# Rounding to eight bits on unscaled values in a fused attention and feed-forward kernel: block floors and limits in bf16, and set places for GpSimd's sums

## The chip, the cores and the metric

The kernel runs on one core of a Trainium2 chip. The metric is the device time of the whole program in microseconds (us); less is better. The engines of the core run at the same time, each through its own list of instructions in order, and wait for each other at semaphores: TensorE (PE), VectorE (DVE), ScalarE (ACT), GpSimd (POOL) and the queue of SyncE (SP), which issues most transfers.

## The reference, cut to what matters

```python
x = x + attn(cond(x, weights, itok_B_0_15), Wqkv, bqkv, Wo, bo)    # x: 64 x 32 x 512
x = x + ffn(gated(x, itok_B_9_3973, conv_w), weight, bias)

# cond: each batch's 32 channels mixed by one of 16 matrices; attn: softmax over 32 tokens
# gated: a mean over the first `length` columns, 5 taps over the rows, gate = sigmoid, x * gate
def quantize_mx(x2d):                       # rows in blocks of 32 values
    amax = jnp.max(jnp.abs(xb), axis=-1)
    exp = jnp.floor(jnp.log2(jnp.maximum(amax, 1e-38))) - 8
    scale = jnp.exp2(exp)                   # a power of two for each block
    q = jnp.clip(xb / scale[..., None], -448.0, 448.0).astype(jnp.float8_e4m3fn)
    return q, scale
out = dequant(quantize_mx(x)) @ dequant(quantize_mx(weight)).T + bias   # then cast to bf16
```

## The kernel before, in words

The 2048 rows of x (64 batches of 32 channels) are 16 tiles of 128 rows and 512 columns. Two tiles make a unit, so there are eight units (UNITS = 8, SUB = 2). The quantising code works in ten steps, numbered v: v = 0 and 1 are the two halves of the feed-forward weight, v = 2 to 9 are the units 0 to 7.

All engines follow one loop over s that is written out by hand. In pass s, TensorE works on the attention of unit s, the projections of unit s + 1, the mixing of unit s + 2 and the feed-forward product of unit s - 2. Its order in a pass is: transposes of step s, `turn_v(s)`, `project_qk(s + 1, 0)`, `attend(s)`, `mix(s + 2)`, `project_out(s, 0)`, `project_qk(s + 1, 1)`, `project_out(s, 1)`, `scores(s + 1)`, `ffn(s - 2, 0)`, `project_v(s + 1)`, `convolve(s)`, `ffn(s - 2, 1)`. Three of its waits matter here: `attend(s)` (L481) waits for the four transposes `softmax_turn` of VectorE; `project_out(s, 1)` (L498) waits for `x2_done`, VectorE's first `residual_sum` (L855) of the unit, because both halves use one PSUM bank; `convolve(s)` (L505) waits for both `masked_sum` (L864) of VectorE.

ScalarE's order in a pass begins `copy_v(s)`, `magnitude(s + 1, 0)`, `copy_o(s)`, `magnitude(s + 1, 1)`, `copy_transposed(s)`. `copy_o` (L663) waits for `attend`. Before the first pass its order is two `copy_mix`, then `magnitude(0, 0)` and `magnitude(0, 1)`.

Quantising a step before the change: VectorE takes the largest magnitude of each block (`block_max`, L878), multiplies it by the gate (`gated_max`), keeps its exponent bits (`scale_exponent`), makes the block scale (`scale_value`, L916) and its inverse (`scale_inverse`, L923), multiplies the inverse by the gate (`gated_inverse`, L929) and writes the scaled values h (`scaled`, L941). ScalarE writes 2^20 |h| in bf16 (`magnitude`, L656). VectorE rounds h by adding max(2^20 |h|, floor) and taking it away again (`round_sum`, L950; `round_back`, L958), clips (`clip`, L967), and GpSimd multiplies by the block scale (`dequantise`, L373), which gives xq. TensorE transposes xq.

GpSimd has three kinds of sums besides: `bias_low` (L386), `residual` (L363, x plus a bias row, 128 x 1024 in f32) and `final_sum` (L294). In pass s its order is `residual(s)`, `dequantise(s + 1)`, `final_sum(s - 2, 0)`, `final_sum(s - 2, 1)`.

VectorE's matrix for the five taps (`band_matrix`, L801 to L818) lies between `scaled(0, ...)` and `round_sum(0, 0)`. `score_max(0)` (L825) follows the second weight half's `block_max` and scales, and `softmax_inverse(0)` follows it.

## Time and profile before

| | |
|---|---|
| median of 3 runs | 169.82 us (169.04 to 169.82) |
| the profiled execution's own time | 170.97 us |
| its span, first to last instruction | 169.3 us |
| mean granted clock of TensorE | 0.879 of 2.4 GHz |
| busy: PE, DVE, ACT, POOL | 130.5, 134.9, 65.4, 64.6 us |

An engine's busy time counts what its instructions last, waits inside an instruction too. Where an instruction lasts much longer than others of its line and shape, it waited for something after it had been started. A clock of 1.00 is 2.4 GHz and 0.50 is 1.2 GHz. "issue" in the chain is time in which the engine on the chain had nothing that the profile shows as its releaser.

### The profile page before, as it was taken

The numbers are of one execution on the slowest core, as the hardware profiler recorded it, in microseconds if no ns is written. First come the engines' busy times: TensorE is split into PE (matmuls) and PEld (weight loads), VectorE is DVE, ScalarE is ACT, GpSimd is POOL, SyncE is SP. The second block draws the span as 40 slices with busy tenths as digits, with TensorE's granted clock in tenths as the row PEclk, the third lists the DMA queues.
The fourth block names the chain that finished last, engine by engine and source line by source line (L and its number), as shares of the span: only waits on it lengthen the run. The fifth ranks groups of instructions, "written<-read, shape, count | busy, mean of one in ns | idle before, by whom it ended". The sixth has DMA issues, their size and how long they took to land.

```text
span 169.3 us, 2698 instructions
## 1 busy us (share of the span) xinstructions
PE 130.5 (77%) x738; PEld 90.4 (53%) x738; DVE 134.9 (80%) x279; ACT 65.4 (39%) x158; POOL 64.6 (38%) x48
## 2 busy tenths in 40 slices
PE   6902899699679889959994999499929955947492
PEld 2402789586477676647573867376716633323130
DVE  4198299759987989899989797978799699599932
ACT  0110433554552646426451545144523463106321
POOL 5330058005612902580555055505551553254500
PEclk9985559999978999999999699959995996587959
DMA  4979103040400000042016001100110011101033
GB/s 112 330 216 321 41 15 122 4 129 6 129 8 2 0 0 0 12 148 98 4 64 187 9 3 64 62 0 0 66 62 0 0 62 62 46 18 41 25 124 124
DMA packets 9489, 11.49 MB, mean 68 GB/s; under 512 B 3954, under 2 KB 4466, under 8 KB 9474
## 3 DMA queue, kind: packets, MB, share of 16 engines
q1 hardware_dynamic: 7186, 8.62, 15.2%
q10 hardware_dynamic: 2096, 2.64, 4.9%
q0 software_dynamic: 192, 0.05, 0.5%
q8 instruction: 6, 0.10, 0.2%
q14 instruction: 9, 0.07, 0.2%
HBM read 7.12 MB, written 4.19 MB: 67 GB/s over the span
## 4 chain that ended last, share of the span: by engine, by line
PE 65%; issue 13%; DVE 6%; DMA 5%; POOL 3%; ACT 3%; SPq 2%; POOLq 1%; ACTq 0%; DVEq 0%
PE ps_qk L439 17%; PE ps_mix L426 12%; PE ps_wo L498 10%; PE ps_v L450 8%; PE ps_ffn L535 7%; DMA mix_w<-in_L_cond_weights_dram 5%; PE ps_att L481 3%; POOL xq L373 2%; PE ps_ffn L533 2%; PE ps_att L471 2%; DVE inv_g L929 1%; PE ps_v L460 1%; SPq L303 1%; PE ps_tr L517 1%; DVE mix_w L972 1%
## 5 line engine op out<-in xcount | busy, mean ns | idle before, releaser
L373 POOL TENSOR_TENSOR xq<-h_clip,scale 128x1024 bf16<-128x1024 bf16 (+1 forms) x11 | 23.1, 2104 | 55.8 <-DVE h_clip L967 37.3
L439 PE MATMUL ps_qk<-xc,wqkv_f 128*128 128x256 f32 x128 | 33.1, 407 | 0.8 <-ACT xc L648 0.8
L439 PEld LDWEIGHTS ps_qk<-xc,wqkv_f 128*128 128x128 f32 x128 | 26.3, 210 | 9.2 <-issue 5.9
L426 PE MATMUL ps_mix<-mix_w,x_sb 128*128 128x128 f32 x128 | 20.8, 331 | 7.5 <-DMA mix_w<-in_L_cond_weights_dram 7.5
L426 PEld LDWEIGHTS ps_mix<-mix_w,x_sb 128*128 128x128 f32 x128 | 19.7, 242 | 8.0 <-issue 7.9
L656 ACT ACTIVATE h_mag<-h 128x512 bf16<-128x512 f32 x20 | 12.4, 625 | 27.4 <-DVE h L941 27.4
L294 POOL TENSOR_TENSOR result<-ffn_out,x 128x512 f32<-128x512 bf16 x12 | 14.5, 1208 | 20.7 <-ACT ffn_out L715 20.7
L498 PE MATMUL ps_wo<-wo_f,o_t 128*128 128x512 f32 x30 | 19.0, 722 | 1.0 <-ACT o_t L663 1.0
L363 POOL TENSOR_TENSOR xb<-x_sb,bo_row 128x1024 f32<-128x1024 f32 x8 | 19.2, 2397 | 0.0
L950 DVE SCALAR_TENSOR_TENSOR h_sum<-h_mag,h 128x512 f32<-128x512 bf16 x20 | 13.7, 691 | 6.8 <-ACT h_mag L656 5.9
L481 PE MATMUL ps_att<-prob_t,v_sb 128*128 128x128 f32 x32 | 5.9, 311 | 15.9 <-issue 15.9
L535 PE MATMUL ps_ffn<-wq_t,xq_t 128*128 128x512 bf16 x56 | 17.0, 433 | 0.0
L450 PE MATMUL ps_v<-xc,wqkv_f 128*128 128x256 f32 x64 | 15.3, 383 | 0.0
L855 DVE TENSOR_TENSOR x<-ps_wo,xb 128x512 f32<-128x512 f32 x15 | 10.3, 688 | 5.4 <-PE ps_wo L498 5.3
L481 PEld LDWEIGHTS ps_att<-prob_t,v_sb 128*128 128x128 f32 x32 | 4.7, 207 | 18.4 <-issue 18.3
L648 ACT ACTIVATE xc<-ps_mix 128x512 f32<-128x512 f32 x16 | 9.6, 597 | 11.8 <-PE ps_mix L426 11.8
L958 DVE SCALAR_TENSOR_TENSOR h_round<-h_mag,h_sum 128x1024 bf16<-128x1024 bf16 (+1 forms) x11 | 12.4, 1128 | 1.0
L450 PEld LDWEIGHTS ps_v<-xc,wqkv_f 128*128 128x128 f32 x64 | 12.0, 190 | 2.1
L715 ACT ACTIVATE ffn_out<-ps_ffn 128x512 bf16<-128x512 f32 x14 | 8.3, 596 | 12.3 <-PE ps_ffn L535 12.3
L864 DVE SCALAR_TENSOR_TENSOR masked<-pos_f,len_f,x 128x512 f32<-128x512 f32 x16 | 12.9, 805 | 0.0
L671 ACT ACTIVATE q_t<-ps_qk,bq_scaled 128x256 f32<-128x256 f32 x8 | 3.8, 473 | 21.1 <-PE ps_qk L439 21.1
L941 DVE TENSOR_TENSOR h<-x,inv_g 128x512 f32<-128x512 f32 x16 | 11.3, 749 | 0.2
(86 smaller groups left out, 198.0 us busy)
## 6 DMA issues: line engine op xcount, KB each, us to landing
out_dram<-result SPq DMA_DIRECT2D x16, 256.0 KB, 2.0
x_sb<-in_x_dram SPq DMA_DIRECT2D x7, 512.0 KB
ffn_w_f<-in_L_ffn_weight_dram ACTq DMA_DIRECT2D x2, 512.0 KB, 8.6
mix_w<-in_L_cond_weights_dram SPq DMA_DIRECT2D x56, 4.0 KB, 1.6
wqkv_f<-in_L_attn_Wqkv_dram ACTq DMA_DIRECT2D x1, 768.0 KB, 5.4
x_sb<-in_x_dram SPq DMA_DIRECT2D x2, 256.0 KB, 6.4
bias_row<-in_L_ffn_bias_dram ACTq DMA_DIRECT2D x1, 256.0 KB, 5.6
bo_row<-in_L_attn_bo_dram ACTq DMA_DIRECT2D x1, 256.0 KB, 7.6
```

What stands on the lines that cost most here:

```text
L294: engine.tensor_tensor(result[:, t, :], ffn_out[:, t, :], x2[:, u % 3, t, :], ALU.add) \
L363: nc.gpsimd.tensor_tensor(xb[:, u % 2], x_sb[:, u], bo_row[:].to_broadcast([P, SUB, T]), ALU.add) \
L373: nc.gpsimd.tensor_tensor(xq[:, v % 2, t0:t1].rearrange("p t (n k) -> p (t n) k", k=BLOCK), h_clip[:, v % 2, t0:t1].rearrange("p t (n k) - ...
L426: mm = nc.tensor.matmul(ps_mix[t][:, c, :], x_sb[:, u, t, c * P:(c + 1) * P], mix_w[:, u, t, :], start=True, stop=True)
L439: mm = nc.tensor.matmul(ps_qk[:, which, :], wqkv_f[:, c, which * D:(which + 1) * D], xc[:, u % 2, c, :], start=(c == 0), stop=(c == TC - 1))
L450: mm = nc.tensor.matmul(ps_v[:], wqkv_f[:, c, 2 * D:3 * D], xc[:, u % 2, c, :], start=(c == 0), stop=(c == TC - 1))
L481: mm = nc.tensor.matmul(ps_o[:, t * P:(t + 1) * P], v_sb[:, u % 2, t, :], prob_t[:, t, :], start=True, stop=True)
L498: nc.tensor.matmul(wo_bank(u, t), o_t[:, tok], wo_f[:], start=True, stop=True) \
L535: mm = nc.tensor.matmul(bank, xq_t[:, u % 2, c, t * P:(t + 1) * P], wq_t[:, c, :], start=False, stop=(c == TC - 1))
L656: nc.scalar.activation(h_mag[:, v % 2, t, :], h[:, v % 2, t, :], ACT.Abs, scale=ROUND_GAIN).then_inc(h_mag_done, 1)
L864: nc.vector.scalar_tensor_tensor(out=masked[:, t, :], in0=pos_f[:], scalar=len_f[:, i:i + 1], in1=x2[:, u % 3, t, :], op0=ALU.is_lt, op1=A ...
L950: nc.vector.scalar_tensor_tensor(out=h_sum[:, t, :], in0=h_mag[:, v % 2, t, :], scalar=ROUND_FLOOR, in1=h[:, v % 2, t, :], op0=ALU.max, op ...
```

## The change

The values are no longer scaled. With the gate times 2^20 as a new scalar (`gate_gain`), ScalarE takes the magnitude straight from x2 (or from the weight), in an order in which the block index runs fastest: it reads x2 at a step of 32 floats and writes h_mag without gaps. A new `limits` writes, for every block, a floor, an upper and a lower limit in bf16. VectorE then does a maximum of h_mag with the floors (`floor_step`), the sum with the gated x2, again read at a step of 32 floats (`round_sum`), the difference (`round_back`), and two passes for the limits (`clip_high`, `clip_low`), of which the last writes xq. `floor_step`, `clip_high` and `clip_low` have bf16 alone as inputs and outputs; `round_back` now is a tensor_tensor. `scale_value`, `scale_inverse`, `gated_inverse`, `scaled`, `clip` and GpSimd's `dequantise` are gone. In VectorE's order the four transposes of the softmax stand together ahead of the gate's chain, the whole of `quantise(s + 1)` stands ahead of `residual_sum(s, 0)`, `masked_sum` moves to the end of the pass, and `band_matrix` moves behind `quantise(0)`. GpSimd's `residual(0)` directly follows `bias_low(0)`; later sums wait for `prob_n_done` or `xq_done`.

```diff
 pool:
             bias_low(0)
-            dequantise(0)
+            residual(0)
+            bias_low(1)
             for s in range(UNITS - 1):
-                residual(s)
-                dequantise(s + 1)
+                if s >= 3:
+                    pool.wait_ge(prob_n_done, s + 1)
+                    final_sum(nc.gpsimd, s - 3, 1)
+                pool.wait_ge(xq_done, SUB * (s + 2))
+                residual(s + 1)
                 if s >= 2:
                     final_sum(nc.gpsimd, s - 2, 0)
-                if s >= 2:
-                    final_sum(nc.gpsimd, s - 2, 1)
...
-            residual(UNITS - 1)
+            pool.wait_ge(prob_n_done, UNITS)
+            final_sum(nc.gpsimd, UNITS - 4, 1)
+            pool.wait_ge(xq_done, SUB * (UNITS + 1))
             final_sum(nc.gpsimd, UNITS - 3, 0)
-            dequantise(UNITS)
             final_sum(nc.gpsimd, UNITS - 3, 1)
-            dequantise(STEPS - 1, 0, 1)
-            dequantise(STEPS - 1, 1, 2)
 scalar, magnitude(v, t):
-                act.wait_ge(h_done, SUB * v + t + 1)
-                nc.scalar.activation(h_mag[:, v % 2, t, :], h[:, v % 2, t, :], ACT.Abs,
-                                     scale=ROUND_GAIN).then_inc(h_mag_done, 1)
+                if v < WBLOCKS:
+                    act.wait_ge(ffn_w_loaded[v], 16)
+                    src, by = ffn_w_f[:, SUB * v + t, :], ROUND_GAIN
+                else:
+                    act.wait_ge(gain_done, v - WBLOCKS + 1)
+                    src, by = x2[:, (v - WBLOCKS) % 3, t, :], gain[:, t:t + 1]
+                nc.scalar.activation(h_mag[:, v % 2, t, :].rearrange("p (k n) -> p k n", n=NB),
+                                     src.rearrange("p (n k) -> p k n", k=BLOCK), ACT.Abs,
+                                     scale=by).then_inc(h_mag_done, 1)
 vector:
+            def gate_gain(v):
+                nc.vector.tensor_scalar(gain[:], gate[:], ROUND_GAIN, None, ALU.mult)
+            def limits(v):
+                nc.vector.scalar_tensor_tensor(
+                    out=limit[:].rearrange("p a t n -> p a (t n)"),
+                    in0=amax_e[:].rearrange("p t n -> p (t n)").unsqueeze(1)
+                    .to_broadcast([P, 3, SUB * NB]),
+                    scalar=AMAX_FLOOR,
+                    in1=limit_k[:].unsqueeze(2).to_broadcast([P, 3, SUB * NB]),
+                    op0=ALU.max, op1=ALU.mult).then_inc(limit_done, 1)
+            def each_block(which, t0, t1):
+                return limit[:, which, t0:t1].unsqueeze(2).to_broadcast([P, t1 - t0, BLOCK, NB])
+            def floor_step(v, t0=0, t1=SUB):
+                dve.wait_ge(limit_done, v + 1)
+                dve.wait_ge(h_mag_done, SUB * v + t1)
+                nc.vector.tensor_tensor(blocks_last(h_floor[:, t0:t1]),
+                                        blocks_last(h_mag[:, v % 2, t0:t1]),
+                                        each_block(0, t0, t1), ALU.max)
+            def round_sum(v, t):
+                nc.vector.scalar_tensor_tensor(
+                    out=h_sum[:, t, :].rearrange("p (k n) -> p k n", n=NB),
+                    in0=src.rearrange("p (n k) -> p k n", k=BLOCK), scalar=by,
+                    in1=h_floor[:, t, :].rearrange("p (k n) -> p k n", n=NB),
+                    op0=ALU.mult, op1=ALU.add).then_inc(h_sum_done, 1)
+            def round_back(v, t0=0, t1=SUB):
+                nc.vector.tensor_tensor(h_round[:, t0:t1], h_sum[:, t0:t1], h_floor[:, t0:t1],
+                                        ALU.subtract)
+            # clip_high: h_min = min(h_round, each_block(1)); clip_low: xq = max(h_min, each_block(2))
             scale_exponent(0)
-            scale_value(0)
-            scale_inverse(0)
-            scaled(0, 0)
-            scaled(0, 1)
+            limits(0)
+            quantise(0)
             band_matrix()
-            round_sum(0, 0)
-            round_sum(0, 1)
-            round_back(0)
-            clip(0)
             block_max(1, 0)
             block_max(1, 1)
+            score_max(0)
             scale_exponent(1)
-            scale_value(1)
-            scale_inverse(1)
-            score_max(0)
...
             for s in range(UNITS - 1):
                 softmax_inverse(s)
                 softmax_divide(s)
+                for j in range(JB):
+                    softmax_turn(s, j)
                 if s + 1 >= WBLOCKS:
+                    gate_chain(s + 1)     # denominator, value, gain, gated_max, exponent, limits
+                quantise(s + 1)           # floor_step, 2 round_sum, round_back, clip_high, clip_low
                 residual_sum(s, 0)
-                clip(s + 1)
-                masked_sum(s, 0)
                 block_max(s + WBLOCKS, 0)
                 residual_sum(s, 1)
+                block_max(s + WBLOCKS, 1)
                 score_max(s + 1)
+                masked_sum(s, 0)
                 masked_sum(s, 1)
-                block_max(s + WBLOCKS, 1)
```

In the last pass and behind it the same steps stand in the same order, with step 9 done in two halves.

## Rows read from the trace of the kernel before

**Rows 1.** Windows from one attend to the next; busy us and count by engine, PEclk.
```profile
34.14:47.81 13.67, 10.69 (x77) 8.22 (x76) 11.55 (x26) 6.59 (x17) 5.75 (x3) 1.00 0.26 82
47.81:61.47 13.66, 12.56 (x77) 10.03 (x77) 11.87 (x29) 6.58 (x17) 5.06 (x2) 0.88 0.02 3
61.47:76.55 15.08, 12.83 (x87) 9.35 (x87) 13.98 (x29) 7.04 (x18) 6.92 (x4) 1.00 0.17 55
76.55:91.84 15.29, 12.83 (x86) 9.34 (x87) 13.95 (x29) 7.03 (x18) 6.92 (x4) 1.00 0.22 66
91.84:108.57 16.73, 14.43 (x86) 10.81 (x87) 13.85 (x29) 7.04 (x18) 6.92 (x4) 0.90 0.16 55
...
125.32:141.55 16.23, 11.21 (x62) 7.18 (x63) 13.94 (x29) 6.87 (x17) 6.91 (x4) 0.87 0.09 32
```

**Rows 2.** The chain that ended last: start us, us, what.
```profile
30.10 0.24 DVE negmax L825
...
42.20 0.13 PE ps_wo L505 x2
...
45.35 2.46 issue
...
74.36 2.19 issue
...
89.44 2.40 issue
```

**Rows 3.** Timeline, a lone `gated_inverse` and one beside GpSimd: start us, us.
```profile
60.90 0.19 DVE L929 TENSOR_TENSOR inv_g<-inv,gate 128x32 f32<-128x32 f32 x1
...
73.79 2.34 POOL L363 TENSOR_TENSOR xb<-x_sb,bo_row 128x1024 f32<-128x1024 f32 x1
73.90 2.27 DVE L929 TENSOR_TENSOR inv_g<-inv,gate 128x32 f32<-128x32 f32 x1
```

**Rows 4.** Timeline, from attend to the first rounding sum, and a first residual sum.
```profile
34.62 0.38 ACT L663 ACTIVATE o_t<-ps_att 128x256 f32<-128x256 f32 x1 [1.27 <-PE ps_att L481]
34.91 0.62 ACT L656 ACTIVATE h_mag<-h 128x512 bf16<-128x512 f32 x1
...
65.58 0.68 DVE L855 TENSOR_TENSOR x<-ps_wo,xb 128x512 f32<-128x512 f32 x1
```

**Rows 5.** Groups of VectorE and ScalarE: busy us, mean ns, idle before.
```profile
L950 DVE SCALAR_TENSOR_TENSOR h_sum<-h_mag,h 128x512 f32<-128x512 bf16 x20 | 13.7, 691 | 6.8 <-ACT h_mag L656 5.9
L864 DVE SCALAR_TENSOR_TENSOR masked<-pos_f,len_f,x 128x512 f32<-128x512 f32 x16 | 12.9, 805 | 0.0
L958 DVE SCALAR_TENSOR_TENSOR h_round<-h_mag,h_sum 128x1024 bf16<-128x1024 bf16 x9 | 11.0, 1225 | 0.9
L878 DVE TENSOR_REDUCE amax<-x 128x16 f32<-128x512 f32 x16 | 10.8, 679 | 0.0
L967 DVE TENSOR_SCALAR h_clip<-h_round 128x1024 bf16<-128x1024 bf16 x9 | 4.5, 504 | 0.1
```

**Rows 6.** A copy of ScalarE with 1024 columns, same view.
```profile
L708 ACT ACTIVATE xq_t<-ps_tr 128x1024 bf16<-128x1024 bf16 x7 | 7.1, 1018 | 0.3 <-PE ps_tr L517 0.3
```

**Rows 7.** Conversions that read every fourth word: ns min/median/max.
```profile
L790 DVE CAST len_f<-len_i x4: 161/166/1362, 7.9 to 8.5; 32x16 f32<-32x16 int32 x4
```

**Rows 8.** Timeline before the first attend.
```profile
14.36 0.17 DVE L801 MEMSET same<- 128x128 f32 x1
17.55 0.29 DVE L818 TENSOR_TENSOR band<-band_k,same 128x128 f32<-128x128 f32 x1
20.77 0.62 ACT L656 ACTIVATE h_mag<-h 128x512 bf16<-128x512 f32 x1
22.71 1.83 POOL L386 TENSOR_TENSOR bias_rest<-bias_row,bias_part 128x512 f32<-128x512 f32 x1 [12.87 <-ACT bias_part L629]
```

**Rows 9.** Timeline of the last step.
```profile
154.74 0.62 ACT L656 ACTIVATE h_mag<-h 128x512 bf16<-128x512 f32 x1
...
159.72 1.43 POOL L373 TENSOR_TENSOR xq<-h_clip,scale 128x512 bf16<-128x512 bf16 x1 [0.23 <-DVE h_clip L967]
```

More of the change, by code:

```diff
@@ L927, in gated_inverse @@
[L927 to L936 removed]
+            def gate_gain(v):
+                u = v - WBLOCKS
+                dve.wait_ge(gate_done, u + 1)
+                if u >= 1:
+                    dve.wait_ge(h_mag_done, SUB * v)
+                nc.vector.tensor_scalar(gain[:], gate[:], ROUND_GAIN, None, ALU.mult) \
+                    .then_inc(gain_done, 1)
@@ L947, in round_sum @@
-            def round_sum(v, t):
-                dve.wait_ge(h_mag_done, SUB * v + t + 1)
-                nc.vector.scalar_tensor_tensor(out=h_sum[:, t, :], in0=h_mag[:, v % 2, t, :],
-                                               scalar=ROUND_FLOOR, in1=h[:, v % 2, t, :],
-                                               op0=ALU.max, op1=ALU.add) \
-                    .then_inc(h_sum_done, 1)
+                    src, by = x2[:, (v - WBLOCKS) % 3, t, :], gate[:, t:t + 1]
+                nc.vector.scalar_tensor_tensor(
[3 more added lines that the diff above has]
+                    op0=ALU.mult, op1=ALU.add).then_inc(h_sum_done, 1)
@@ new lines, in clip_high, with clip_low @@
+            def clip_high(v, t0=0, t1=SUB):
+                dve.wait_ge(h_round_done, SUB * v + t1)
+                nc.vector.tensor_tensor(blocks_last(h_min[:, t0:t1]),
+                                        blocks_last(h_round[:, t0:t1]),
+                                        each_block(1, t0, t1), ALU.min) \
+                    .then_inc(h_min_done, t1 - t0)
+            def clip_low(v, t0=0, t1=SUB):
+                dve.wait_ge(h_min_done, SUB * v + t1)
+                if v >= 2:
+                    dve.wait_ge(tr_done, SUB * (v - 1))
+                nc.vector.tensor_tensor(blocks_last(xq[:, v % 2, t0:t1]),
+                                        blocks_last(h_min[:, t0:t1]),
+                                        each_block(2, t0, t1), ALU.max) \
+                    .then_inc(xq_done, t1 - t0)
@@ L971, in _, with quantise, gate_chain @@
+            def quantise(v):
+                floor_step(v)
+                round_sum(v, 0)
+                round_sum(v, 1)
+                round_back(v)
+                clip_high(v)
+                clip_low(v)
+            def gate_chain(v):
+                gate_denominator(v)
+                gate_value(v)
+                gate_gain(v)
+                gated_max(v)
+                scale_exponent(v)
+                limits(v)
             nc.vector.memset(warm[:], 0.0).then_inc(warm_zeroed, 1)
@@ L972, in _ @@
             nc.vector.memset(mix_w[:], 0.0).then_inc(mix_w_zeroed, 1)
+            for a, value in enumerate((FLOOR_PER_POWER, CEIL_PER_POWER, -CEIL_PER_POWER)):
+                nc.vector.memset(limit_k[:, a:a + 1], value).then_inc(limit_k_done, 1)
             lengths()
@@ L1048, in _ @@
             masked_sum(UNITS - 1, 0)
-            clip(UNITS)
             masked_sum(UNITS - 1, 1)
+            clip_high(UNITS)
+            clip_low(UNITS)
             block_max(STEPS - 1, 0)
             block_max(STEPS - 1, 1)
-            gate_denominator(UNITS + 1)
-            gate_value(UNITS + 1)
-            gated_max(UNITS + 1)
-            scale_exponent(UNITS + 1)
-            scale_value(UNITS + 1)
-            scale_inverse(UNITS + 1)
-            gated_inverse(UNITS + 1)
-            scaled(STEPS - 1, 0)
-            scaled(STEPS - 1, 1)
-            round_sum(STEPS - 1, 0)
-            round_back(STEPS - 1, 0, 1)
-            round_sum(STEPS - 1, 1)
-            clip(STEPS - 1, 0, 1)
-            round_back(STEPS - 1, 1, 2)
-            clip(STEPS - 1, 1, 2)
+            gate_chain(UNITS + 1)
+            for t in range(SUB):
+                floor_step(STEPS - 1, t, t + 1)
+                round_sum(STEPS - 1, t)
+                round_back(STEPS - 1, t, t + 1)
+                clip_high(STEPS - 1, t, t + 1)
+                clip_low(STEPS - 1, t, t + 1)
             for u in (UNITS - 2, UNITS - 1):
```

123 lines of the change are left out of this document (27 added, 96 removed).

## The prediction

> **What bounds the kernel now.** I read the windows first, cut from one `attend` (L481) to the next, so that each window is one pass of the loop [rows 1]. The reader is to see that TensorE is busy for 12.8 of 15.1 us at the full clock in a pass that has everything in it, and VectorE for 14.0. So both are nearly full, and the question is who waits for whom. The chain that ended last [rows 2] answers it: it runs along TensorE, with one gap in each pass, 2.46 us in pass 0 and 2.19 us in pass 2, each directly before `attend`, which needs VectorE's four transposes. The timeline shows why they are late [rows 3]: `gated_inverse`, which stands between the transposes, takes 0.19 us alone and 2.27 us when GpSimd's residual sum (2.34 us) started just before it; it ends when that sum ends. I call this the lock: a VectorE instruction with two SBUF inputs waits for a running GpSimd sum.
>
> The gap can cost twice. After gaps of 2.46 us (pass 0) and 2.40 us (pass 3) TensorE's granted clock falls to the lower of its two levels, 1.2 GHz, for a while, and passes 1 and 4 run at a mean of 0.88 and 0.90; after the 2.19 us at 74.36 pass 3 keeps 1.00 [rows 1, 2]. Pass 5 repeats pass 4, and pass 6 has 0.87, so four passes had a fall. I price one at 16.73 - 15.08 = 1.65 us [rows 1].
>
> **Part 1, the transposes go together.** Nothing of the gate stands between them any more, so the old gap of 2.2 us is gone from before `attend`. What is late next is the first residual sum, since the whole of `quantise(s + 1)` now stands ahead of it in VectorE's order and `project_out(s, 1)` waits for it. I follow the ring from one `attend` (time a) to the next:
> - `attend` 0.68, then `copy_o` and, queued behind it, `magnitude(s + 1, 1)`: 34.62 to 35.53 is 0.91 [rows 4]. With the hand-over, a + 1.62.
> - `floor_step` waits for it. Its price is that of a bf16 pass over 1024 columns with two inputs, which the trace lacks. From below it is the clip's 0.50 (one input), from above `h_round`'s 1.23 (an input in f32) [rows 5]. I take the sum over 512 columns, 0.69, as if two bf16 columns counted as one.
> - Two `round_sum` at 0.69, `round_back` 1.23, `clip_high` and `clip_low` 0.69 each, `residual_sum` 0.68 [rows 4, 5]. With the floor 5.36, so x2 is there at a + 6.98.
> - From the end of x2 (66.26 [rows 4]) to the point where TensorE was ready for the next `attend` (74.36 [rows 2]) are 8.10 us.
>
> The ring is 6.98 + 8.10 = 15.1 us, against 15.08 before. A wait of about 2.2 us before `project_out(s, 1)` takes the place of the one removed. The gate's own chain and `limits` lie beside `attend` and the magnitudes.
>
> In passes 0 and 1, which have no feed-forward product, `convolve(s)` is last: behind x2 stand a block maximum 0.68, the second residual sum held by TensorE (to a + 8.9), 0.68 again, `score_max` 0.2 and two masked sums of 0.75, to a + 11.2 [rows 5]. From `convolve` (42.20) to the end of what precedes `attend` (45.35) are 3.15 us [rows 2]. The pass takes 14.4 us; before it took 13.67, and 13.66 less a clock fall, 12.0 [rows 1].
>
> **Part 2, reads at a step of 32 floats.** `round_sum` and `magnitude` now read one float in every 128 bytes. The only such row has 16 elements at every fourth word and shows no cost beside its fixed time, 0.16 us [rows 7]; an extra 10 ns in it would not be seen, and over 512 elements that is 0.3 us. From below the cost is nothing; from above each element counts as two, which is 1225 - 691 = 0.53 us for `round_sum` [rows 5] and 1.02 - 0.62 = 0.40 for `magnitude` [rows 4, 6]. I take half of the upper end, 0.27 and 0.21, because the small row allows about that much. The ring has two `round_sum` and one `magnitude`: +0.75 in each pass.
>
> The Trainium skill has a rule on this (Vector Engine (DVE) Microarchitecture Reference, Measured stream behaviour on trn2): a port keeps its rate only for pairs of adjacent words, and one source that hops at every element ran at 1.73 ns per column against 1.05. By it `round_sum` would rise by about 0.35 us, an estimate from that page, and the sum for the kernel would be some 2 us above mine. No row here has such a read that is long enough.
>
> **Part 3, the beginning.** `magnitude(0, 1)` ends at 21.4 [rows 8], with the step at 21.8. VectorE filled the time before it with `band_matrix`, 14.36 to 17.84, 3.5 us [rows 8]; now that comes behind. After 21.8: `quantise(0)` 0.69 + 2 x 0.96 + 1.23 + 2 x 0.69 = 5.2. Into it falls GpSimd's `bias_low(0)`, released at 22.71 [rows 8] (its 1.83 us hold a wait; about 1.1 clean, half of a residual), and `residual(0)` of 2.34 [rows 3] right behind it; nearly all passes of `quantise` have two SBUF inputs, so 3.4 us of lock are added. Then `band_matrix` 3.5 and two block maxima 1.35. `score_max(0)` starts at 35.2; before, at 30.10, and there it lay on the chain [rows 2]. ScalarE's `exp_scores(0)` stands ahead of the copies that TensorE needs, so the delay of 5.1 us passes on whole. TensorE is idle for over 5 us meanwhile, so one clock fall of 1.65 comes with it. Together +6.75.
>
> **Part 4, the end.** In the last step `magnitude` starts behind a copy at 154.7 as before. It takes 0.62 + 0.21, and each half then two `round` steps of 0.96 and 0.69 and three bf16 passes over 512 columns at 0.43 (0.16 fixed and half of 0.53): 2.94. Both halves end at 161.4, where GpSimd's product ended at 161.15 [rows 9]: +0.25. GpSimd's product of 1.43 at the end is paid back by VectorE's passes.
>
> **The sum.** Beginning +6.75. Passes 0 and 1: 2 x (14.4 + 0.75) = 30.3 against 25.7, +4.6, and +0.7 where `residual(1)` locks the gate's chain; the clock would fall in both, but only 0.7 of each fall shows, since `convolve` waits for VectorE there, and one whole fall was there before: -0.25. Passes 2 to 5: +0.75 each, +3.0. Their wait is 15.85 - 12.83 = 3.0 us, longer than the gaps after which the clock fell; two of the four had a fall before, and I count three, +1.65. Pass 6 has no `project_qk` before `attend` and is held by the transposes at about 14.3 and a fall, as before (16.23 [rows 1]): 0. End +0.25. Together 6.75 + 4.6 + 0.7 - 0.25 + 3.0 + 1.65 + 0.25 = 16.7 us. The profiled execution took 170.97 (span 169.3), so it would take 187.7. The median of the runs shown is 1.15 lower, 169.82, and gives 186.5.
>
> **Rivals.**
> - *The step is free* (0.22). Part 2 falls out: beginning +5.8, passes 0 and 1 +3.6, passes 2 to 6 nothing, end -1.05. That is +8.3, 178, or down to 173 where three of the clock's falls stay away. For it speaks the small row [rows 7], against it that it is small.
> - *The ring's wait becomes too short for the clock to fall* (0.26), which ends on the fast side. Its place is the wait before `project_out(s, 1)`. If the step is free and a bf16 pass costs 0.50, as the clip does [rows 5], the ring is 14.5 us and the wait 1.7, less than the 2.19 that kept the clock once. From +8.3 come off 3 x 0.19 in seven passes (4.0), 0.6 in the beginning and 5.0 for three falls (passes 4, 5, 6): -1.3, 168.5, and lower as far as `residual(0)` misses `quantise(0)` (3.4), 165. It decides from a ring of about 14.8 us downwards.
> - *A hopping read costs a whole column or more* (0.14). The ring is 16.6, every pass has its fall: +16.7 + 1.0 in the beginning + 5.3 + 1.65, some 194.
> - My forecast (0.38), 181 to 191.
>
> Runs of this kernel tell 0.5% (0.85 us) from no change, and no less. Faster is the second rival, 0.22, but for 0.04 of it that lies within 0.5%; the rest, 0.74, is slower. The range of 166 to 193 leaves out the lower end of the second rival and the upper half of the third.
>
> **What would show it.** In the profile after: `score_max(0)` at 34 to 36 us instead of 30.1, with long VectorE passes beside GpSimd's at 23 to 29; TensorE's gap before the second `project_out` and not before `attend`; `round_sum` near 0.96 and `magnitude` near 0.83; `floor_step` and the limits near 0.69 (at 1.2 the ring grows by 1.6, past my range). It is wrong if the steps are free and the gap stays under 2 us, or if `residual(0)` finds other work than `quantise(0)`.

## The result, and the profile of the changed kernel

The changed kernel takes 196.77 us (median of 4 runs, 196.56 to 201.03), the kernel before on the same chip 169.43 (168.68 to 169.82): a ratio of 1.162, 95% interval [1.155, 1.168]. Some executions of a kernel run at a lower granted clock and take longer (the 201.03 here, at 0.829 instead of 0.842); the ratios leave them out. The profiled execution took 196.96 us with a span of 195.3, against 170.97 and 169.3. So the direction was right, and the size was not: 186.5 was forecast, and 196.8 lies above the range that ended at 193.

The span grew by 26.0 us where 16.7 were forecast. The starts of the `attend` groups cut it into three parts: the first starts at 41.11 instead of 33.98 (+7.1, forecast 6.75), the seven passes take 123.7 instead of 107.6 (+16.2, forecast 9.7), and from the last `attend` to the end it is 30.46 instead of 27.75 (+2.7, forecast 0.25).

The windows from one `attend` to the next, in the columns of [rows 1], and the stretch behind the last one:

```profile
41.11:57.51 16.40, 12.55 (x78) 9.68 (x77) 11.72 (x27) 7.51 (x18) 1.47 (x2) 0.90 0.13 36
57.51:74.89 17.38, 13.29 (x77) 9.73 (x76) 11.85 (x27) 8.26 (x18) 4.48 (x2) 0.80 0.00 1
74.89:93.00 18.11, 14.42 (x87) 10.24 (x86) 12.28 (x27) 8.38 (x19) 4.67 (x3) 0.91 0.04 15
93.00:110.98 17.98, 14.30 (x87) 9.71 (x86) 13.21 (x27) 8.16 (x18) 4.68 (x3) 0.91 0.20 61
110.98:130.38 19.40, 15.71 (x87) 10.65 (x86) 12.30 (x28) 8.16 (x18) 4.67 (x3) 0.82 0.19 57
...
148.35:164.84 16.49, 11.04 (x63) 6.46 (x61) 11.98 (x26) 6.04 (x16) 3.93 (x3) 0.90 0.08 32
164.84:195.30 30.46, 18.16 (x64) 7.61 (x64) 20.04 (x37) 11.49 (x17) 3.34 (x3) 0.78 0.16 61
```

The reader is to see three things. VectorE is busy for 12 to 13 us of a pass and no longer for 14, though the passes are longer. That is not work saved: the 13.98 us of the third row of [rows 1] hold about 3 us in which VectorE was held by GpSimd (`gated_inverse` 2.27 instead of 0.19 [rows 3], `scale_inverse` 0.94 instead of 0.18, the two masked sums 0.3 more), and its own work in a pass rose by about 1 us: 2.35 us of scaling, inverses and `clip` went, 2.50 of gain, floor and limits came, and the two `round_sum` grew by 0.8. TensorE's granted clock is below 1.00 in all seven passes, where it was in four. And no engine is full in any pass, so they wait for each other.

For whom, the groups of instructions say (busy us, mean ns | idle before, releaser), beside [rows 5]:

```profile
L483 PE MATMUL ps_wo<-wo_f,o_t 128*128 128x512 f32 x30 | 20.1, 759 | 27.1 <-DVE x L846 26.5 <-ACT o_t L654 0.5
L646 ACT ACTIVATE h_mag<-x,gain 128x512 bf16<-128x512 f32 x16 | 18.8, 1183 | 0.1
L946 DVE SCALAR_TENSOR_TENSOR h_sum<-x,gate,h_floor 128x512 f32<-128x512 f32 x16 | 17.0, 1098 | 0.3
L955 DVE TENSOR_TENSOR h_round<-h_sum,h_floor 128x1024 bf16<-128x1024 f32 x9 | 11.0, 1226 | 0.9
L934 DVE TENSOR_TENSOR h_floor<-h_mag,limit 128x1024 bf16<-128x1024 bf16 x9 | 6.2, 693 | 36.2 <-ACT h_mag L646 36.2
L960 DVE TENSOR_TENSOR h_min<-h_round,limit 128x1024 bf16<-128x1024 bf16 x9 | 6.2, 692 | 0.8
L646 ACT ACTIVATE h_mag<-ffn_w_f 128x512 bf16<-128x512 f32 x4 | 4.2, 1075 | 0.0
```

TensorE waits 26.5 us in all before `project_out` (L483) for the first residual sum. In the kernel before the same group waited 1.0 us:

```profile
L498 PE MATMUL ps_wo<-wo_f,o_t 128*128 128x512 f32 x30 | 19.0, 722 | 1.0 <-ACT o_t L663 1.0
```

VectorE waits 36.2 us for ScalarE's magnitudes. The new bf16 passes take the 0.69 us that were taken for them. The two readers at a step of 32 floats are the surprise: 1.18 us for the magnitude (0.83 was forecast, 0.62 is [rows 4]) and 1.10 for `round_sum` (0.96 was forecast).

One pass as a timeline, from the `attend` at 110.98 (start us, us):

```profile
111.63 0.38 ACT L654 ACTIVATE o_t<-ps_att 128x256 f32<-128x256 f32 x1 [0.72 <-PE ps_att L466]
111.91 1.19 ACT L646 ACTIVATE h_mag<-x,gain 128x512 bf16<-128x512 f32 x1
...
113.23 0.69 DVE L934 TENSOR_TENSOR h_floor<-h_mag,limit 128x1024 bf16<-128x1024 bf16 x1 [2.22 <-ACT h_mag L646]
...
113.95 2.13 DVE L946 SCALAR_TENSOR_TENSOR h_sum<-x,gate,h_floor 128x512 f32<-128x512 f32 x2
...
116.19 1.23 DVE L955 TENSOR_TENSOR h_round<-h_sum,h_floor 128x1024 bf16<-128x1024 f32 x1
...
117.52 0.69 DVE L960 TENSOR_TENSOR h_min<-h_round,limit 128x1024 bf16<-128x1024 bf16 x1
118.31 0.69 DVE L969 TENSOR_TENSOR xq<-h_min,limit 128x1024 bf16<-128x1024 bf16 x1
118.91 0.68 DVE L846 TENSOR_TENSOR x<-ps_wo,xb 128x512 f32<-128x512 f32 x1
...
119.65 2.08 PE L483 MATMUL ps_wo<-wo_f,o_t 128*128 128x512 f32 x2 [3.69 <-DVE x L846]
```

This is the ring of Part 1, link by link. x2 is there at a + 8.61 (119.59) and not at a + 7.73: the magnitude has 0.36 more than forecast, the two sums 0.21 more, and the last 0.3 are spaces of about 0.1 between an instruction and the one that reads its whole output (116.08 to 116.19, 117.42 to 117.52, 118.21 to 118.31), which I had not counted. Behind the wait of 3.69 us two products take 2.08 us instead of the 1.12 that they take in experiment 3 at a clock of 1.00: the clock has fallen to its lower level.

The beginning, as in [rows 8]:

```profile
22.77 0.69 DVE L934 TENSOR_TENSOR h_floor<-h_mag,limit 128x1024 bf16<-128x1024 bf16 x1 [10.39 <-ACT h_mag L646]
23.49 4.85 DVE L946 SCALAR_TENSOR_TENSOR h_sum<-ffn_w_f,h_floor 128x512 f32<-128x512 f32 x2
...
31.24 0.17 DVE L792 MEMSET same<- 128x128 f32 x1
...
35.83 0.21 DVE L816 TENSOR_REDUCE negmax<-ps_att 128x2 f32<-128x64 f32 x1
...
23.24 1.24 POOL L373 TENSOR_TENSOR bias_rest<-bias_row,bias_part 128x512 f32<-128x512 f32 x1 [13.39 <-ACT bias_part L614]
24.44 3.05 POOL L363 TENSOR_TENSOR xb<-x_sb,bo_row 128x1024 f32<-128x1024 f32 x1
```

The two `round_sum` take 4.85 us beside GpSimd's two sums (23.24 to 27.49), `band_matrix` starts at 31.24 behind the quantising, and `score_max(0)` at 35.83, against 30.10 in [rows 2].

### The profile page after: what moved, and what is told of

It is laid out like the page before. It is cut to its first block and busy times, and to the rows that moved or that the text cites. A ratio compares the mean times of both kernels' runs of the same rounds, so it can differ in the third digit from the quotient of the medians.

```text
span 195.3 us, 2690 instructions
## 1 busy us (share of the span) xinstructions
PE 137.7 (71%) x738; PEld 90.8 (46%) x738; DVE 127.5 (65%) x274; ACT 76.0 (39%) x158; POOL 41.3 (21%) x37
## 5 line engine op out<-in xcount | busy, mean ns | idle before, releaser
L483 PE MATMUL ps_wo<-wo_f,o_t 128*128 128x512 f32 x30 | 20.1, 759 | 27.1 <-DVE x L846 26.5
L934 DVE TENSOR_TENSOR h_floor<-h_mag,limit 128x1024 bf16<-128x1024 bf16 (+1 forms) x11 | 7.1, 644 | 38.5 <-ACT h_mag L646 38.5
L435 PE MATMUL ps_v<-xc,wqkv_f 128*128 128x256 f32 x64 | 20.0, 469 | 0.0
L483 PEld LDWEIGHTS ps_wo<-wo_f,o_t 128*128 128x128 f32 x30 | 5.1, 214 | 30.6 <-DVE x L846 29.3
L646 ACT ACTIVATE h_mag<-x,gain 128x512 bf16<-128x512 f32 x16 | 18.8, 1183 | 0.1
L435 PEld LDWEIGHTS ps_v<-xc,wqkv_f 128*128 128x128 f32 x64 | 15.7, 250 | 4.1 <-issue 1.1
L946 DVE SCALAR_TENSOR_TENSOR h_sum<-x,gate,h_floor 128x512 f32<-128x512 f32 x16 | 17.0, 1098 | 0.3
L955 DVE TENSOR_TENSOR h_round<-h_sum,h_floor 128x1024 bf16<-128x1024 f32 (+1 forms) x11 | 12.4, 1129 | 1.0
L624 ACT ACTIVATE prob<-ps_att,negmax 128x32 f32<-128x32 f32 x16 | 4.4, 284 | 19.1 <-DVE negmax L816 19.1
L402 PE MATMUL ps_att<-warm 128*128 128x512 bf16 x34 | 10.4, 470 | 1.3 <-DVE warm L990 1.3
L869 DVE TENSOR_REDUCE amax<-x 128x16 f32<-128x512 f32 x16 | 10.9, 685 | 0.5
```

What stands on the lines that cost most here:

```text
L435: mm = nc.tensor.matmul(ps_v[:], wqkv_f[:, c, 2 * D:3 * D], xc[:, u % 2, c, :], start=(c == 0), stop=(c == TC - 1))
L483: nc.tensor.matmul(wo_bank(u, t), o_t[:, tok], wo_f[:], start=True, stop=True) \
L646: nc.scalar.activation(h_mag[:, v % 2, t, :].rearrange("p (k n) -> p k n", n=NB), src.rearrange("p (n k) -> p k n", k=BLOCK), ACT.Abs, sca ...
L869: nc.vector.tensor_reduce(amax[:, v % 2, t, :], src[:, t, :].rearrange("p (n k) -> p n k", k=BLOCK), AX.X, ALU.max, apply_absolute_value=T ...
L946: nc.vector.scalar_tensor_tensor(out=h_sum[:, t, :].rearrange("p (k n) -> p k n", n=NB), in0=src.rearrange("p (n k) -> p k n", k=BLOCK), s ...
L955: nc.vector.tensor_tensor(h_round[:, t0:t1], h_sum[:, t0:t1], h_floor[:, t0:t1], ALU.subtract).then_inc(h_round_done, t1 - t0)
```

## The experiments

A single span scatters by one or two us, mostly in the start (the first `floor_step` begins between 20.9 and 23.1 in different runs), so I compare passes and stretches where I can. Unless it is said otherwise the edit is to the changed kernel.

**1. Both readers without the step.**

```diff
-nc.scalar.activation(h_mag[:, v % 2, t, :].rearrange("p (k n) -> p k n", n=NB),
-                     src.rearrange("p (n k) -> p k n", k=BLOCK), ACT.Abs,
+nc.scalar.activation(h_mag[:, v % 2, t, :], src, ACT.Abs,
...
-    out=h_sum[:, t, :].rearrange("p (k n) -> p k n", n=NB),
-    in0=src.rearrange("p (n k) -> p k n", k=BLOCK), scalar=by,
-    in1=h_floor[:, t, :].rearrange("p (k n) -> p k n", n=NB),
+    out=h_sum[:, t, :], in0=src, scalar=by, in1=h_floor[:, t, :],
```

> The changed kernel with the step of 32 floats taken out of both readers: magnitude and round_sum read x2 and write without gaps, so the block limits fall on the wrong elements; nothing else is changed. Theory A (the step costs about 0.3 to 0.4 us in each round_sum and 0.5 us in each magnitude, and these lie on the ring): round_sum 0.69, magnitude 0.63 to 0.7, each pass shorter by 1.1 to 1.3 us, beginning and end by about 1.4 us each, span 184 to 185 instead of 195.3, and less if falls of the clock go too. Theory B (the step is small and the excess over the prediction is the clock's): under 4 us gained, round_sum stays near 1.0.

Measured: 182.97 us, ratio to before 1.083 [1.073, 1.093], span 180.7. The magnitude takes 0.717 and `round_sum` 0.749. So the step is worth 14.6 of the 26.0 us by the two spans (13.8 by the medians), somewhat more than expected: 1.6 ahead of the first `attend`, 9.7 in the passes, 3.4 behind the last one. The other 11.4 us come with the rest of the change, the new order and the new instructions; experiment 9 shows that another order gives them back. One pass kept the full clock, and in it the next wait can be seen (window, then the timeline in it):

```profile
71.43:87.68 16.25, 13.00 (x87) 9.31 (x86) 13.06 (x27) 7.23 (x18) 4.69 (x3) 1.00 0.05 17
```

```profile
82.19 1.16 POOL L294 TENSOR_TENSOR result<-ffn_out,x 128x512 f32<-128x512 bf16 x1 [1.50 <-ACT ffn_out L705]
...
82.19 1.71 DVE L854 SCALAR_TENSOR_TENSOR masked<-pos_f,len_f,x 128x512 f32<-128x512 f32 x1
...
83.96 0.38 PE L490 MATMUL ps_wo<-ysum,band 128*128 128x2 f32 x2 [0.76 <-DVE masked L854]
```

The second `masked_sum` takes 1.71 us instead of 0.75 beside one of GpSimd's final sums, and `convolve` waits 0.76 us for it. The lock that was moved away from the transposes is back one step later.

**2. The step in ScalarE's magnitude alone** (`round_sum` as in experiment 1).

> The changed kernel with the step of 32 elements read by ScalarE's magnitude alone; round_sum reads its floor without a step, at the wrong elements. The run without either step had a span of 180.7 us, the changed kernel 195.3. Theory (both readers lie on the ring, each counts with its own difference): the magnitude costs 0.46 more (1.18 against 0.72) and the two round_sum 0.35 each (1.10 against 0.75), 1.16 us in a pass; the magnitude's share is 0.46 in a pass, 3.2 us over seven passes and about 1 more in the beginning, to 184 to 187 with the clock falls it brings. Rival (the magnitude alone makes the wait before the second project_out long enough for the clock to fall in every pass): 190 or more, with a granted clock below 0.85. Other rival (the magnitude is hidden behind VectorE's own work): 181 to 182.

Measured: 190.36 us, span 188.6, 7.9 more than without any step, clock 0.846. The span lies between theory and rival: it is under 190, but what the rival named did happen, a fall in every pass and a mean clock below 0.85. The parts say why. In the passes that have one clock fall in both kernels it is 17.27 against 16.80 us: 0.47, the magnitude's own difference. The changed kernel has 17.97 there, 0.70 more, which is twice `round_sum`'s 0.35. So both readers lie on the ring and each counts with just what it grew by. The rest came with the clock: the one pass that had kept 1.00 (16.25 us) now has 0.82 (18.51), and the end grows by 2.7 us, of which 1.3 lie behind the last xq, where the last feed-forward product now runs at the lower level (1.91 us instead of 1.03).

**3. TensorE kept busy in the wait.** Fourteen products with zeros ahead of the second `project_out`.

```diff
 project_qk(s + 1, 1)
+keep_warm(14)
 project_out(s, 1)
```

> The changed kernel with 14 products of zeros (128x512, result not used) on TensorE between project_qk(s + 1, 1) and project_out(s, 1), where it waits 3.7 us for the first residual sum. Theory A (the wait makes the clock fall, and the fall costs 1.2 to 2.7 us in each pass after it): the granted clock stays at 1.00 behind the wait, project_out to attend takes 8.1 us instead of 9.3 to 10.8, span 185 to 188. Rival (the products delay project_out, or VectorE binds the passes): span 194 to 197.

Measured: 191.15 us, span 189.5; the window of one pass and, in it, `convolve`'s wait:

```profile
91.34:108.78 17.44, 16.02 (x101) 10.68 (x100) 13.71 (x27) 8.16 (x18) 4.69 (x3) 1.00 0.20 64
```

```profile
103.35 1.65 DVE L856 SCALAR_TENSOR_TENSOR masked<-pos_f,len_f,x 128x512 f32<-128x512 f32 x1
...
105.06 0.38 PE L490 MATMUL ps_wo<-ysum,band 128*128 128x2 f32 x2 [0.77 <-DVE masked L856]
```

All seven passes have 1.00. So the fall of the clock comes from the wait in which TensorE has nothing to do, and it costs 5.7 us over the passes (123.7 to 118.0); where the changed kernel has one short fall (0.91) it is only 0.5 us in a pass, and 1.9 in the pass at 0.82. The span is neither the 185 to 188 of the theory, which took a fall to cost 1.2 us or more, nor the rival's. This run also gives the ring at the full clock: 17.44 us, against 16.25 without the step (experiment 1). The difference is 1.19, and 0.46 + 2 x 0.35 is 1.16.

**4 and 5. The beginning.** `band_matrix` ahead of `quantise(0)` (4), and besides GpSimd's `residual(0)` held until xq of step 0 is written (5).

```diff
 limits(0)
-quantise(0)
 band_matrix()
+quantise(0)
...
 bias_low(0)
+pool.wait_ge(xq_done, SUB)              # experiment 5 only
 residual(0)
```

> The changed kernel with band_matrix back ahead of quantise(0), and residual(0) left right behind bias_low(0). Theory A (the order costs 3.5 us and the lock about 3 us, and they add): score_max(0) starts at 32.3 us instead of 35.8, first attend 3.5 us earlier, the pair of first rounding sums still lasts 4.8 us. Rival (the lock alone holds it): first attend moves by under 1 us.

> The changed kernel with band_matrix back ahead of quantise(0) and GpSimd's residual(0) held until xq_done of step 0. Theory A (order and lock delay score_max(0), and the delay passes on whole): score_max(0) starts at 29 to 30 us instead of 35.8, the first round_sum pair takes about 2 us instead of 4.85, the first attend comes 6 to 7 us earlier, span 188 to 189.5. Rival: TensorE's copies and loads bind the beginning, the first attend comes less than 2 us earlier.

Measured: 190.69 us (span 189.0) and 192.06 (span 190.4). From `floor_step(0)` to `score_max(0)` it is 13.06 us in the changed kernel, 9.57 in (4) and 7.54 in (5): the order is worth 3.5 us and the lock of `residual(0)` 2.0. In (5), with the sums beside `bias_low` alone:

```profile
23.71 2.79 DVE L947 SCALAR_TENSOR_TENSOR h_sum<-ffn_w_f,h_floor 128x512 f32<-128x512 f32 x2
...
30.53 0.22 DVE L817 TENSOR_REDUCE negmax<-ps_att 128x2 f32<-128x64 f32 x1
```

The first `attend` comes at 34.63 and 35.06. In (4) that is 6.5 us earlier and not 3.5: 1.6 us are the earlier start, and 1.4 a shorter way from `score_max(0)` to `attend` (3.9 us instead of 5.3). The clock makes those: TensorE waits 2.24 us there and not 5.30, the granted clock of the stretch is 1.00 and not 0.55, and eight products ahead of `attend` take 1.89 us (4) instead of 3.10 (changed kernel):

```profile
32.91 1.89 PE L424 MATMUL ps_qk<-xc,wqkv_f 128*128 128x256 f32 x8
...
38.17 3.10 PE L424 MATMUL ps_qk<-xc,wqkv_f 128*128 128x256 f32 x8
```

The passes of (5) take 125.6 us together instead of 123.7, with more of them at a clock of 0.82 (19.2 and 19.4 us), so a beginning that is 6 us shorter shows 5 to 6 in the span.

**6. `magnitude(s + 1, 1)` ahead of `copy_o(s)`**, so that it no longer waits for `attend`.

```diff
 magnitude(s + 1, 0)
-copy_o(s)
 magnitude(s + 1, 1)
+copy_o(s)
```

> The changed kernel with ScalarE's magnitude(s + 1, 1) ahead of copy_o(s). Theory A (a ring runs attend, copy_o, magnitude, VectorE's six passes, residual sum, project_out, attend): floor_step no longer waits for attend, starts 1.5 to 2 us earlier, TensorE's wait before the second project_out falls from 3.7 to about 2, steady passes 16 to 16.8 instead of 18, span 184 to 188. Rival (VectorE's own load binds a pass, not the ring): passes stay near 18, span 193 or more.

Measured: 186.35 us, span 184.7, passes 113.4 together. Passes at the full clock have 16.35 to 16.63 us instead of 17.44. The magnitude had indeed been queued on ScalarE behind a copy that waits for TensorE.

**7. The first residual sum directly behind the two `round_sum`.**

```diff
-quantise(s + 1)
+floor_step(s + 1); round_sum(s + 1, 0); round_sum(s + 1, 1)
 residual_sum(s, 0)
+round_back(s + 1); clip_high(s + 1); clip_low(s + 1)
```

> The changed kernel with residual_sum(s, 0) of VectorE moved ahead of round_back, clip_high and clip_low of the same pass. Theory A (the ring closes through the first residual sum): x2 is there 2.8 us earlier, the wait before the second project_out falls from 3.7 to about 0.9, the clock stays up, steady passes 15 to 16, span 178 to 183. Rival (the time is moved to a later wait, convolve or attend, since VectorE has the same work): passes 17 or more, span 190 or more.

Measured: 193.95 us, span 192.3, 3 us less than the changed kernel; a pass at the full clock has 16.75 us instead of 17.44. The second product, the locks and the convolution of one pass:

```profile
98.64 1.13 PE L483 MATMUL ps_wo<-wo_f,o_t 128*128 128x512 f32 x2 [0.76 <-DVE x L846]
...
103.69 1.61 POOL L294 TENSOR_TENSOR result<-ffn_out,x 128x512 f32<-128x512 bf16 x1
...
104.22 1.63 DVE L855 SCALAR_TENSOR_TENSOR masked<-pos_f,len_f,x 128x512 f32<-128x512 f32 x1
...
105.91 0.59 PE L490 MATMUL ps_wo<-ysum,band 128*128 128x2 f32 x2 [2.97 <-DVE masked L855]
```

The wait before `project_out` falls from 3.7 to 0.76, and `convolve` waits 2.97 instead, since VectorE has the same work to do ahead of the masked sums: the rival's case. Its two products take 0.59 us instead of 0.28, so in this pass (clock 0.91) the clock falls there now. Not every such wait does this: in the two passes behind it `convolve` waits the same 2.97 us and the clock stays at 1.00. An instruction brought forward helps only if what stands behind it isn't awaited as well.

**8. The whole computation without a step.** The limits are written twice, side by side, and read in pairs of bf16, so that all values stay in their natural order and no reader steps.

```diff
-limit = sb("limit", [P, 3, SUB, NB], BF16)
+limit = sb("limit", [P, 3, SUB, NB, 2], BF16)
...
-return limit[:, which, t0:t1].unsqueeze(2).to_broadcast([P, t1 - t0, BLOCK, NB])
+return limit[:, which, t0:t1].rearrange("p t n b -> p (t n) b").unsqueeze(2) \
+    .to_broadcast([P, (t1 - t0) * NB, BLOCK // 2, 2])
```

> The whole computation of the changed kernel in the natural order of elements: no read has a step, and each block limit is stored twice in bf16, so that the limit is read as a pair of neighbours, 16 times over. limits becomes two instructions of 0.26 us. Theory A: floor_step and the clips stay near 0.69 us, round_sum 0.69, magnitude 0.65; span within 1 us of the kernel without the step, 184 to 186. Rival (a limit read in pairs loses the double rate): floor_step and clips 1.2 us, each pass longer by 1.5, span 193 to 196.

Measured: 185.3 us, ratio 1.097 [1.086, 1.107], span 181.4; a pass at the full clock has 16.27 us, as in experiment 1. The floors' passes keep their 0.69 us, so the order with the block index fastest wasn't needed for it:

```profile
L935 DVE TENSOR_TENSOR h_floor<-h_mag,limit 128x1024 bf16<-128x1024 bf16 x9 | 6.2, 693 | 24.6 <-ACT h_mag L646 24.6
```

**9. Experiments 8, 5, 6 and 7 in one kernel.**

> The changed kernel's computation without a step (limits stored in pairs), band_matrix first, residual(0) after quantise(0), magnitude ahead of copy_o and the first residual sum ahead of round_back. Theory A (these parts are the whole of the loss): first attend at 34, passes 13.5 to 15, span 163 to 168, at or under the kernel before. Rival (locks of VectorE by GpSimd's sums and VectorE's load keep passes near 16): span 174 or more.

Measured: 169.47 us (10 runs), ratio 1.004 [0.991, 1.016], span 166.4. The changed kernel is back at the time before. `convolve` still waits, 20.0 us in all, for the masked sums at the end of VectorE's pass.

**10. The same, with each masked sum behind its residual sum** and the block maxima at the end.

```diff
 residual_sum(s, 0)
+masked_sum(s, 0)
 round_back(s + 1)
-clip_high(s + 1); clip_low(s + 1)
-block_max(s + WBLOCKS, 0)
 residual_sum(s, 1)
-block_max(s + WBLOCKS, 1)
+masked_sum(s, 1)
 score_max(s + 1)
-masked_sum(s, 0); masked_sum(s, 1)
+clip_high(s + 1); clip_low(s + 1)
+block_max(s + WBLOCKS, 0); block_max(s + WBLOCKS, 1)
```

> As the run with all parts (no step, limits in pairs, band first, residual(0) later, magnitude ahead of copy_o), with another order of VectorE in passes 0 to 6: floor, two sums, first residual and masked sum, round_back, second residual and masked sum, score_max, the two limits, the block maxima. Theory A (what is left in each pass is convolve waiting 2.2 us for masked sums that GpSimd's sums lock, and the clock that falls after it): that wait goes, passes 13.5 to 14.5, span 152 to 158. Rival (VectorE's work and locks fill the pass): passes stay at 15 to 16.8, span 164 or more.

Measured: 160.21 us, ratio 0.954 [0.946, 0.962], span 157.1: faster than both kernels. A steady pass, and the locks left in it:

```profile
86.06:100.38 14.32, 13.06 (x86) 9.41 (x87) 12.95 (x29) 7.35 (x18) 4.59 (x4) 1.00 0.24 78
```

```profile
96.77 2.36 POOL L363 TENSOR_TENSOR xb<-x_sb,bo_row 128x1024 f32<-128x1024 f32 x1 [9.73 <-DVE xq L969]
...
97.98 1.23 DVE L826 TENSOR_TENSOR prob_n<-prob,prob_inv 128x64 f32<-128x64 f32 x1
99.09 2.27 POOL L294 TENSOR_TENSOR result<-ffn_out,x 128x512 f32<-128x512 bf16 x2
...
100.31 1.08 DVE L878 TENSOR_SCALAR gate_den<-eg 128x2 f32<-128x2 f32 x1
```

The two block maxima (one input) lie beside the first half of the residual sum and are not held; `prob_n` (two inputs) takes 1.23 us until that sum ends, where it has 0.55 in the passes of the changed kernel and 0.23 at its beginning.

**11. Experiment 10 with the step and the single limits of the changed kernel.**

> The same order with the reads at a step of 32 floats kept as in the changed kernel. Theory A (the step costs what it lies on): once the ring is open, its 1.2 us in each pass is hidden in part, span 3 to 8 us above the run without the step. Rival (the step costs the same 14 us as in the changed kernel, because VectorE is full): span 12 or more above.

Measured: 174.12 us, ratio 1.031 [1.024, 1.038], span 173.2; a pass at the full clock has 15.92 us instead of 14.32. So the step costs about 14 us in this order too (13.9 by the medians, 16.1 by the two profiled executions, one of them the slowest of its runs and the other the fastest), which is the rival's case. In each pass VectorE stands still for both magnitudes:

```profile
96.22 2.23 ACT L647 ACTIVATE h_mag<-x,gain 128x512 bf16<-128x512 f32 x2 [3.44 <-DVE gain L909]
...
98.58 0.69 DVE L935 TENSOR_TENSOR h_floor<-h_mag,limit 128x1024 bf16<-128x1024 bf16 x1 [1.84 <-ACT h_mag L647]
```

They start at the gain, which stands behind the transposes, so the magnitudes and the sums lie one after another in VectorE's own time for a pass, and this order doesn't hide them.

**12. Experiment 10 with other places for GpSimd's final sums and for VectorE's block maxima.**

```diff
-pool.wait_ge(prob_n_done, s + 1)
-final_sum(nc.gpsimd, s - 3, 1)
+pool.wait_ge(gain_done, s)
+final_sum(nc.gpsimd, s - 3, 0); final_sum(nc.gpsimd, s - 3, 1)
 pool.wait_ge(xq_done, SUB * (s + 2))
 residual(s + 1)
-if s >= 2:
-    final_sum(nc.gpsimd, s - 2, 0)
...
 for j in range(JB): softmax_turn(s, j)
+block_max(s + 1, 0); block_max(s + 1, 1)       # no longer at the end of the pass
 gate_chain(s + 1)
```

> The version with pairs, its beginning in the other order and the masked sums right behind the residual sums (span 157.1), with the block maximum of the next step moved behind the transposes and ahead of the gate chain, and both final_sum of GpSimd waiting for VectorE's gain of the step. Theory: prob_n (1.22) and gate_den (1.08) are long there because GpSimd holds the port pair that they want; with the sums moved they fall to their short length (0.2 to 0.6), passes of 13.0 to 13.6 instead of 14.33, span 149 to 155. Rival: the hold moves on to the quantising of the gain, the floor or the limits of the next step, each of them on the same ring, and the time is the same or longer, 157 to 161.

Measured: 168.13 us (12 runs), ratio 0.994 [0.990, 0.999], span 166.4: 8 us worse than experiment 10, beyond even the rival. Of the 9.3 us between the two spans 5.9 lie in the passes. The hold moved on:

```profile
71.44 2.35 POOL L363 TENSOR_TENSOR xb<-x_sb,bo_row 128x1024 f32<-128x1024 f32 x1 [12.24 <-DVE xq L969]
...
71.47 2.40 DVE L826 TENSOR_TENSOR prob_n<-prob,prob_inv 128x64 f32<-128x64 f32 x1
...
76.87 1.14 DVE L900 TENSOR_SCALAR amax_e<-amax_g 128x32 uint32<-128x32 uint32 x1
```

`gate_den` is short now (0.16), as expected. But the block maxima had been what lay beside the residual sum; without them `prob_n`, ahead of `attend`, takes its whole 2.40 us.

**13. The kernel before with its transposes together** (and nothing else of the change).

> The kernel before with one part of the change alone: the four transposes of the softmax stand together ahead of the gate's chain in passes 0 to 6; the old rounding, dequantise and GpSimd's order stay. Theory A (the gap before attend goes, and TensorE then waits a little for the first residual sum): passes 14 to 15 instead of 15.1 to 16.7, span 163 to 167. Rival (the locked gate chain only moves behind the transposes and holds the first residual sum as long): passes 15 or more, span 169 to 171.

Measured: 167.02 us, ratio 0.986 [0.977, 0.994], span 163.0. The lock moves on to the next of the scale's instructions, and passes 3 to 5 stay at 15.1 us (pass 2 takes 12.9), but passes 2 to 5 all have a clock of 1.00 now:

```profile
102.66 2.36 POOL L363 TENSOR_TENSOR xb<-x_sb,bo_row 128x1024 f32<-128x1024 f32 x1
102.78 2.28 DVE L916 TENSOR_SCALAR scale<-amax_e 128x32 f32<-128x32 f32 x1
```

**14. Besides, GpSimd's residual sum for the next pass directly behind its dequantising product.**

```diff
 dequantise(0)
+residual(0)
 for s in range(UNITS - 1):
-    residual(s)
     dequantise(s + 1)
+    residual(s + 1)
```

> The kernel before with the four transposes together and with GpSimd's residual(s + 1) directly behind dequantise(s + 1) instead of at the start of the next pass. Theory A (a sum of 2.3 us that starts while VectorE takes block maxima and transposes locks less): the 2.3 us lock of the gate's chain goes, passes 13.5 to 14.5, span 156 to 160. Rival (the lock only moves to masked_sum and softmax_divide and delays convolve): passes at 15, span 162 or more.

> The kernel before with its two transposes together and the residual sum of the next step's second half right behind the quantising, once more, for an interval: span 157.6 in its first run, median 160.2. Theory: 158 to 161, ratio 0.93 to 0.96, beside the same 160 of the version with pairs, so what gives the gain is the order and not the bf16 limits. Rival: the first run was a lucky one and the median lies at 165 or more.

Measured: 160.23 us at first (four runs, of which one took 184.68, so I give no ratio), then 159.03 (6 runs), ratio 0.938 [0.932, 0.945]. A steady pass has 14.0 us:

```profile
86.61:100.60 13.99, 13.01 (x88) 9.47 (x86) 13.20 (x28) 7.04 (x18) 7.30 (x4) 1.00 0.25 80
```

So the kernel before gains at least as much by two moves, with its scaled values and its dequantising product, as the new computation does at its best (experiment 10).

## Why the prediction was wrong, point by point

- **Part 1, the ring: right in its links, 1.0 us too short (0.3 + 0.7).** The wait before `attend` went and one before the second `project_out` came, of 3.7 us (3.0 forecast), and `floor_step`, `round_back` and the limits took their forecast 0.69, 1.23 and 0.69. Missing were the spaces of 0.1 us behind full passes (0.3), and what follows x2: I took its 8.10 us over from before, but at the full clock it is 17.44 - 8.61 = 8.83. The difference is `convolve`'s 0.77 for a masked sum that GpSimd's final sum holds, as experiments 1 and 3 show. I had moved the masked sums to the end of the pass for passes 0 and 1 and not for the others. Against the kernel before, passes 0 and 1 together are 6.3 us longer (5.05 forecast), passes 2 to 5 9.6 (4.65) and pass 6 0.3 (0).
- **Part 2, the step: the step of the prediction that failed.** "I take half of the upper end, 0.27 and 0.21, because the small row allows about that much" rested on a row of 16 elements. Measured are 0.35 for `round_sum` (1.10 against 0.75, experiment 1) and 0.46 for the magnitude, above its upper end of 0.40, and 0.10 besides for its scale, now one value for each partition (0.717 against 0.62). In a pass 1.26 us instead of 0.75 at the forecast's places. The case "step free" was forecast at +8.3 and measured, in experiment 1, at +11.4; the step itself at +8.4 and measured at +14.6. So of the 9.3 us missing in the sum, 6.2 are the step (5.4 with the medians' 13.8) and 3.1 the rest, which is a balance: the spaces and `convolve`'s wait, less the falls of the clock that were priced too high. The Trainium skill's rule that I weighed (Vector Engine (DVE) Microarchitecture Reference, Measured stream behaviour on trn2) gives 0.35 us for `round_sum`, and the trace agrees: 0.35. It is about VectorE; the larger part for one instruction was ScalarE's.
- **The clock: the cause right, the price too simple.** Experiment 3 shows that the falls come from the wait. There are falls in all seven passes, as against four, but in passes 2 to 5 they cost 73.5 - 69.8 = 3.7 us, no more than the 3.5 before (63.8 - 4 x 15.08): a TensorE that then waits for VectorE anyway loses 0.5 us by a short fall and not 1.65. The +1.65 there should have been about 0; the ring alone gave 69.8 - 60.3 = 9.5 instead of 3.0. Nor does the length of the wait alone decide, as I had assumed: waits of 2.49 us (experiment 1), 2.57 to 2.59 (experiment 6) and 2.97 (experiment 7) were followed by a fall in some passes and not in others.
- **Part 3, the beginning: right, partly by luck.** `score_max(0)` was forecast at 35.2 and came at 35.83; `band_matrix` is 3.5 us, as experiment 4 measures; from there to the first `attend` it is 1.4 more than before (1.65 forecast), the clock's fall as experiment 4 shows. The quantising lasted 8.47 us (8.6 forecast), but the two locks were 4.85 - 2.13 = 2.7 us of it (2.0 by `residual(0)`, experiment 5) and not 3.4, and the step and the spaces made up for that. The first `floor_step` came 1.0 later than forecast, of which the two magnitudes explain 0.5.
- **Part 4, the end: +2.7 instead of +0.25.** The last magnitude starts 14.71 us after the last `attend` instead of 13.19 [rows 9], of which 1.1 are the masked sums that end later; I had it "as before". From it to the last xq it is 7.57 us instead of 6.41; 6.7 was forecast.
- **The rivals.** The measured time is nearest to the third one (a hopping read costs a whole column, 194), and that is what the magnitude's did. The second, on the fast side, came true in no part: even without any step the wait before the second `project_out` was 2.49 us in the steady passes, and six of seven passes had a clock below 1.00. The fixed places of GpSimd's sums didn't end the locks: experiments 1, 7, 10 and 12 each show one, at four different instructions, as experiment 13 does without fixed places. A rule of the Trainium skill fits this (SBUF — State Buffer, Who interferes with whom): a VectorE instruction with two SBUF inputs, or a tensor_scalar in its two-port mode, and a GpSimd instruction that reads SBUF want one port pair, and the second to come waits for the whole of the first. The trace agrees (`prob_n`, two inputs, 2.40 us beside 2.35; `gate_den`, a tensor_scalar, 1.08 beside GpSimd's result), and no block maximum, a reduction of one input, lasted over 0.69 us in any of these runs. The prediction had only the first half of this in view, since it called a lock an affair of two inputs. The trace of the kernel before already spoke against that: beside the residual sum of 88.87 to 91.21 it was a tensor_scalar with one input that was held.

```profile
89.25 2.00 DVE L923 TENSOR_SCALAR inv<-scale 128x32 int32<-128x32 int32 x1
```

What stays open: why the clock falls in some passes and not in others with the same wait, and further in some than in others (0.91 and 0.82 with 3.7 us); and whether the end alone could be brought back. Neither was tried.

## What to carry to other kernels

Price an access pattern that the trace doesn't show at the upper end if it lies on the ring, and look for a layout that avoids it: here pairs of bf16 limits kept the double rate and saved the step on both engines. Before moving a block of work on a loaded engine, list every instruction that another engine awaits in a pass; a wait removed in one place comes back at the next of them, unless what stands between is work that nobody awaits. A lock between two engines is best given a partner that it can't hold (here the block maxima beside the residual sum), and two such moves alone gave the kernel before 6%.
